# A graph network layer on one core: another order of columns for the product of W2 and x

## The chip, the cores and the metric

The kernel runs on one core of one Trainium2 chip. The metric is the device time of one execution in microseconds (us); lower is better.

## The reference, cut to what matters

```python
def _bn(h, gamma, beta):
    mu = jnp.mean(h, axis=0, keepdims=True)
    var = jnp.mean((h - mu) ** 2, axis=0, keepdims=True)
    return (h - mu) * jax.lax.rsqrt(var + EPS) * gamma + beta
row, col = (edge_index[0], edge_index[1])
h = jnp.concatenate([x[row], edge_attr], axis=1)
h = jax.nn.relu(_bn(h @ W1 + b1, g1, be1))
s = jax.ops.segment_sum(h, col, num_segments=n)
agg = jnp.where(cnt > 0, s / jnp.maximum(cnt, 1.0), 0.0)
h2 = jnp.concatenate([x, agg], axis=1)
h2 = jax.nn.relu(_bn(h2 @ W2 + b2, g2, be2))
return jax.nn.relu(h2 @ Wl + bl)          # then: layernorm(x + this)
```

x is 3125 x 128 (nodes), there are 53125 edges with 64 attributes each, sorted by destination, W1 is 192 x 128, W2 is 256 x 256 and Wl is 256 x 128, all in float32. The first 128 rows of W2 meet x, the last 128 meet the mean over edges. The part of the product with x does not depend on the edges at all, so it can be made at any time.

## The kernel before, in words

The edges are cut into 104 groups of 512 (4 tiles of 128). Four groups make a step, so there are 26 steps (i = 0 to 25). A first pass over the 26 steps makes h @ W1 for every edge and the sums for the first norm; a second pass applies the norm's shift and relu and sums into the nodes; a last part does the node layer. This change touches only the first pass.

**One step i of the first pass.** GpSimd (POOL, function `gather`, line 682) fetches rows of the table x @ W1 from DRAM, one indirect DMA for each tile of 128 edges. In group q = 2 three of the four tiles are not fetched but picked by TensorE, so a step from i = 1 on has 13 indirect DMAs and not 16. Before the gathers of group g, GpSimd waits until h of group g - 4 is made (`pool.wait_ge(h_ready, g - 3)`), so it may run at most four groups ahead of the groups that VectorE finishes. GpSimd has nothing else in this pass.

TensorE (PE, function `edge_step`) issues, in this order: the edge product of group 1 (line 766); five products of one-hot matrices with the node table (`pick`, line 784, ten matmuls each), of which the first stands ahead of the change's matmul and the second right behind it; **the x product** (`x_product`, line 847) in steps 1 to 14; the edge products of groups 2 and 3; the counts (line 839), which wait until ScalarE has copied the x product out (they use the same PSUM bank `psT[1]`); the last pick; and `rows_back` (line 793), which adds the picked rows into group 2. Before `rows_back` ScalarE must copy the picked rows out of PSUM (line 1084).

VectorE (DVE) makes h of each group from the product and the gathered rows (line 1306; lines 1303 and 1304 for group 2), adds it to a running sum (line 1327), adds its squares (line 1334), makes three of the five one-hot matrices of a step (line 1319) and the small one-hots for the counts (line 1284).

ScalarE (ACT) squares h of each group (line 1031), makes the other two one-hot matrices of a step (lines 1094, five times, and 1097; `node_hot`), copies the x product out (`x_product_out`, line 1045), starts its DMA to DRAM (line 1047), places counts (line 1059) and copies the picked rows (line 1084).

**The x product.** `xt0` holds x turned, 128 features on the partitions and 3125 columns. They lie as 25 blocks t of 125 columns p (node number = 25 p + t). The result is wanted in node order, p outer and t inner. `XSTEPS` has 14 pieces: 7 ranges of p (six of 20 and one of 5) for each of the 2 halves of W2. A piece has 20 x 25 = 500 columns (5 x 25 = 125 in the last two). A float32 matmul shows as two records in the profile. The pieces are read again from DRAM in the last part.

```python
XP = 20
XSTEPS = [(h, k, min(XP, PN - k)) for k in range(0, PN, XP) for h in range(H2)]
xtv = xt0.rearrange("f (t p) -> f t p", t=NT)      # NT = 25, PN = 125
h2x = agg[:, 3 * GF:3 * GF + XW]                   # XW = 500
```

`psT`, `psH`, `psC`, `psS` and `psX` are PSUM banks; `agg`, `res` and `work` are places in SBUF that several things share.

Of the kernel before, what the change touches and what calls it, by code (L numbers as in the profile page):

```python
# [31 lines left out]
ACT = mybir.ActivationFunctionType  # L32
AX_X = mybir.AxisListType.X

P = 128
# [21 lines left out]
def gnn_kernel(nc, E, x, xt, src, src_rows, dst, dst_rows, ea, W1, b1, g1, be1, W2, b2, g2, be2, Wl, bl, out):  # L57
# [3 lines left out]
    NT = 25  # L61
# [25 lines left out]
    with ctx:  # L87
# [3 lines left out]
        def pb(name, shape):  # L91
            return ctx.enter_context(nc.psum_tensor(name, shape, F32))

        def sem(name):
            return ctx.enter_context(nc.semaphore(name))
# [116 lines left out]
        w2x = agg[:, 0:H2 * P]  # L212
        h2x = agg[:, 3 * GF:3 * GF + XW]
# [5 lines left out]
        psT = [pb(f"psT{i}", [P, 512]) for i in range(2)]  # L219
# [73 lines left out]
        x_ps = sem("w2_x_psum")  # L293
        x_out = sem("w2_x_copied")
# [84 lines left out]
        def slot(i, par, q):  # L379

            return resg(i, q) if q < KEEP else away[par][:, (q - KEEP) * GF:(q - KEEP + 1) * GF]
# [350 lines left out]
        def _(pe):  # L732
# [7 lines left out]
            xtv = xt0.rearrange("f (t p) -> f t p", t=NT)  # L740

            LISTS = len(BATCH) - 1
            for b, (t0, n) in enumerate(BATCH):
# [7 lines left out]
                for t in range(n):  # L751
                    last = pe.matmul(psY[b % len(psY)][0:PN, t * F:(t + 1) * F], xtv[:, t0 + t, :], w1x[:, :],
                                     start=True, stop=True)
# [89 lines left out]
            def x_product(m):  # L843

                h, k, n = XSTEPS[m]
                pe.wait_ge(cnt_placed, m + 1)
                pe.matmul(psT[1][:, 0:n * NT].rearrange("o (p t) -> o p t", t=NT), w2x[:, h * P:(h + 1) * P],  # L847
                          xtv[:, :, k:k + n].rearrange("f t p -> f p t"), start=True, stop=True).then_inc(x_ps, 1)

            def edge_step(i, par, nth):  # L850
                product(i, par, nth, 1)
                if i in NODES:
                    pick(i, 0)
                if i <= len(XSTEPS):
                    x_product(i - 1)
                if i in NODES:
                    pick(i, 1)
                product(i, par, nth, 2)
                if i in NODES:
                    pick(i, 2)  # L860
                    pick(i, 3)
                product(i, par, nth, 3)
                counts(i, par)
                if i in NODES:
                    pick(i, 4)
                    rows_back(i)
                if i + 1 < NI:
                    product(i + 1, 1 - par, (i + 1) // 2 + 1, 0)
# [32 lines left out]
            for j in range(TILES):  # L901
                h = slot(NI - 1, 1, U - 1)[:, j * F:(j + 1) * F]
# [31 lines left out]
            with pe.Else():  # L934
# [3 lines left out]
                          stop=True).then_inc(g_base, 1)  # L938
                with pe.Fori(0, NG) as g:
                    with pe.Fori(0, NB) as b:  # L940
                        pe.wait_ge(g_m, g + 1)
                        pe.wait_ge(g_hot, NB * g + b + 1)
                        for j in range(TILES):
                            pe.matmul(psH[0][:, 0:WIDE], mx[:, 0, j * F:(j + 1) * F], ghot[:, j * WIDE:(j + 1) * WIDE],
                                      start=(j == 0), stop=(j == TILES - 1))
# [8 lines left out]
            for h in range(H2):  # L954
                last = pe.matmul(psX[:, 2 * F + h:2 * F + h + 1], w2[:, h * P:(h + 1) * P], c(C_U), start=True,
                                 stop=True)
            last.then_inc(s_w2s, 1)
            prods = [(n, h) for n in range(NC) for h in range(H2)]
            for k, (n, h) in enumerate(prods):
# [5 lines left out]
                if k >= len(BANK):  # L965
                    pe.wait_ge(s_h2, k - len(BANK) + 1)
                pe.matmul(BANK[k % len(BANK)][:, 0:cw], w2[:, h * P:(h + 1) * P], agg[:, c0:c0 + cw], start=True,
                          stop=True).then_inc(s_h2ps, 1)
# [12 lines left out]
            for b, (t0, n) in enumerate(BATCH):  # L981
                pe.wait_ge(s_h2r, b + 1 if b < DVE_RELU else H2 * (b + 1) - DVE_RELU)
                pe.wait_ge(s_h2rd, min(b + 1, DVE_RELU))
                for t in range(n):
                    o = BANK[b][0:PN, t * F:(t + 1) * F]
                    for h in range(H2):
                        n0 = h * N + (t0 + t) * PN
                        last = pe.matmul(o, h2r[:, n0:n0 + PN], wl[:, h * F:(h + 1) * F], start=False,
                                         stop=(t == n - 1 and h == H2 - 1))
# [4 lines left out]
        def _(act):  # L994
# [44 lines left out]
            def x_product_out(m):  # L1039

                h, k, n = XSTEPS[m]
                act.wait_ge(x_ps, m + 1)
                if m:
                    act.wait_ge(x_saved, 16 * m)
                act.activation(h2x[:, 0:n * NT], psT[1][:, 0:n * NT], ACT.Copy).then_inc(x_out, 1)
                act.wait_ge(x_out, m + 1)
                act.dma_start(h2x_dram[:, h, k * NT:(k + n) * NT], h2x[:, 0:n * NT]).then_inc(x_saved, 16)

# [50 lines left out]

            node_hot(NODE0, 0)  # L1100
            x_product_out(0)
            node_hot(NODE0, 1)
            for i in range(1, NI - 1):
                squares(i, 0)
                place_counts(i)
                if i in NODES:
                    rows_out(i)
                squares(i, 1)
                hot_out(i + 1, (i + 1) % 2)
                if i + 1 in NODES:  # L1110
                    node_hot(i + 1, 0)
                squares(i, 2)
                if i < len(XSTEPS):
                    x_product_out(i)
                squares(i, 3)
                if i + 1 in NODES:
                    node_hot(i + 1, 1)
# [503 lines left out]
```

## Time and profile before

| what | value |
|---|---|
| runs of the kernel before | 586.23, 587.31, 763.84 us (median 587.31) |
| the profiled execution's own time | 585.97 us |
| its span | 584.2 us |
| PE busy | 527.9 us (90%) |
| PE weight load busy | 464.9 us (80%) |
| DVE busy | 509.0 us (87%) |
| ACT busy | 425.3 us (73%) |
| POOL busy | 362.0 us (62%) |
| first pass | to about 443 us |

The profiled execution took 1.8 us more than its span, which is what lies around the program. Two of the three runs stand within 1.4 us of it; the third is far off and is not used. The busy shares are averages over three very different parts; the first pass must be read by its own rows. Engines are named as in the profile: PE is TensorE, PEld its weight load, DVE VectorE, ACT ScalarE, POOL GpSimd.

### The profile page before, as it was taken

The numbers are of one execution on the slowest core, as the hardware profiler recorded it, in microseconds if no ns is written. First come the engines' busy times: TensorE is split into PE (matmuls) and PEld (weight loads), VectorE is DVE, ScalarE is ACT, GpSimd is POOL, SyncE is SP. The second block draws the span as 40 slices with busy tenths as digits, with TensorE's granted clock in tenths as the row PEclk, the third lists the DMA queues.
The fourth block names the chain that finished last, engine by engine and source line by source line (L and its number), as shares of the span: only waits on it lengthen the run. The fifth ranks groups of instructions, "written<-read, shape, count | busy, mean of one in ns | idle before, by whom it ended". The sixth has DMA issues, their size and how long they took to land.

```text
span 584.2 us, 10621 instructions
## 1 busy us (share of the span) xinstructions
PE 527.9 (90%) x3099; PEld 464.9 (80%) x3099; DVE 509.0 (87%) x719; ACT 425.3 (73%) x850; POOL 362.0 (62%) x464
## 2 busy tenths in 40 slices
PE   3679999999999999999999988898997999999993
PEld 4658878877778878888888877787885999999583
DVE  5796999999999999999999989898986877777787
ACT  2458777887788777888888877678767566666476
POOL 4776777777777777777777777777770333333500
PEclk9789999999999999999999999899999999999997
DMA  7844454455444554444444444354345688775004
GB/s 197 263 142 125 158 161 143 133 162 167 155 140 146 163 166 141 140 145 139 143 145 148 145 150 148 109 148 150 95 121 164 219 252 267 251 253 169 1 1 111
DMA packets 48139, 90.21 MB, mean 154 GB/s; under 512 B 10885, under 2 KB 30260, under 8 KB 48099
## 3 DMA queue, kind: packets, MB, share of 16 engines
q1 hardware_dynamic: 30734, 59.97, 31.2%
q0 software_dynamic: 10912, 22.37, 15.0%
q10 hardware_dynamic: 6453, 7.38, 3.6%
q8 instruction: 19, 0.31, 0.2%
q14 instruction: 21, 0.17, 0.1%
HBM read 66.71 MB, written 22.97 MB: 153 GB/s over the span
## 4 chain that ended last, share of the span: by engine, by line
PE 55%; DVE 20%; issue 8%; POOL 8%; ACT 4%; DMA 3%; DVEq 0%; ACTq 0%; POOLq 0%
PE psT L784 22%; PE psH L923 8%; PE psC L923 8%; POOL res L682 6%; DVE node_hot L1319 6%; PE psH L766 5%; PE psT L847 4%; DVE psX L1334 3%; PE psC L766 2%; DVE res L1306 2%; PE psH L793 1%; DMA res<-ytab,srci 1%; DVE res L1473 1%; POOL res L666 1%; ACT node_rows_turned L1084 1%
## 5 line engine op out<-in xcount | busy, mean ns | idle before, releaser
L682 POOL DMA_INDIRECT res<-ytab,srci x265 | 250.2, 944 | 81.8 <-issue 77.1
L784 PE MATMUL psT<-node_hot,node_table 125*128 125x384 f32 x1250 | 261.9, 358 | 4.5 <-DVE node_hot L1319 3.7
L784 PEld LDWEIGHTS psT<-node_hot,node_table 125*128 125x128 f32 x1250 | 222.3, 191 | 29.5 <-issue 12.5
L1319 DVE TENSOR_TENSOR node_hot<-agg,psC 125x1920 fp32r<-125x1920 int32 x75 | 161.0, 2147 | 0.0
L1094 ACT ACTIVATE node_hot<-agg,nodeid 125x384 fp32r<-125x384 int32 x250 | 131.8, 603 | 8.8 <-PE psT L784 6.6
L1097 ACT ACTIVATE node_hot<-node_hot,ones 125x1920 fp32r<-125x1920 f32 x50 | 95.1, 1902 | 1.6
L1435 DVE TENSOR_TENSOR work<-res,psX 128x512 f32<-128x512 f32 x104 | 70.8, 687 | 20.2 <-PE psH L923 10.1
L707 POOL TENSOR_TENSOR agg<-agg,srci 128x64 f32 x104 | 32.0, 308 | 74.6 <-ACT srci L1161 55.0
L766 PE MATMUL psH<-w1e,work 128*128 128x256 f32 x268 | 70.5, 385 | 6.0 <-DVE res L1304 3.3
L682 POOL DMA_INDIRECT work<-ytab,srci x64 | 60.7, 948 | 23.7 <-issue 16.8
L1334 DVE TENSOR_TENSOR psX<-agg,psX 128x512 f32<-128x512 f32 x103 | 71.1, 690 | 4.4 <-ACT agg L1031 4.3
L766 PEld LDWEIGHTS psH<-w1e,work 128*128 128x128 f32 x268 | 47.6, 189 | 16.0 <-DVE res L1304 7.0
L1031 ACT ACTIVATE agg<-res 128x512 f32<-128x512 f32 x77 | 47.5, 618 | 15.1 <-DVE res L1306 7.7
L1327 DVE TENSOR_TENSOR psS<-res,psS 128x512 f32<-128x512 f32 x77 | 53.6, 696 | 2.7
L923 PE MATMUL psH<-work 128*128 128x128 f32 (+1 forms) x416 | 51.9, 279 | 1.0 <-DVE work L1435 1.0
L923 PE MATMUL psC<-work 128*128 128x128 f32 (+1 forms) x416 | 51.2, 277 | 0.0
L923 PEld LDWEIGHTS psH<-work 128*128 128x128 f32 x416 | 49.6, 196 | 1.2 <-DVE work L1435 1.2
L923 PEld LDWEIGHTS psC<-work 128*128 128x128 f32 x416 | 49.1, 194 | 0.0
L766 PE MATMUL psC<-w1e,work 128*128 128x256 f32 x132 | 35.0, 387 | 3.2 <-DVE res L1304 2.3
L1059 ACT ACTIVATE cnt<-psT 1x64 f32 x104 | 22.4, 215 | 20.4 <-PE psT L839 17.6
L1306 DVE TENSOR_TENSOR res<-psH,res 128x512 f32<-128x512 f32 x42 | 28.7, 683 | 2.7 <-DMA res<-ytab,srci 2.4
L766 PEld LDWEIGHTS psC<-w1e,work 128*128 128x128 f32 x132 | 23.5, 189 | 8.2 <-DVE res L1304 4.1
(222 smaller groups left out, 534.8 us busy)
## 6 DMA issues: line engine op xcount, KB each, us to landing
work<-in_edge_attr SPq DMA_DIRECT2D x26, 512.0 KB, 3.6
res<-spill SPq DMA_DIRECT2D x25, 512.0 KB, 3.6
spill<-work SPq DMA_DIRECT2D x13, 512.0 KB, 2.8
spill<-res SPq DMA_DIRECT2D x12, 512.0 KB, 2.9
agg<-in_src_rows SPq DMA_DIRECT2D x25, 192.0 KB, 3.9
res<-ytab,srci POOLq DMA_INDIRECT x265, 2.6
res<-h2x_dram SPq DMA_DIRECT2D x10, 312.5 KB
h2x_dram<-agg ACTq DMA_DIRECT2D x12, 250.0 KB
```

The costliest lines, as they stand in the source:

```text
L682: pool.indirect_dma_start(rows[:, j * F:(j + 1) * F], None, ytab, bass.IndirectOffsetOnAxis(ap=srci[:, j, g:g + 1], axis=0)).then_inc(gath ...
L766: last = pe.matmul(psP[g % len(psP)][:, b * 2 * F:(b + 1) * 2 * F], ea_cols(par, q, b), w1e[:, :, :].rearrange("p a f -> p (a f)"), start= ...
L784: last = pe.matmul(rows_at, table[0:PN, part, (t0 + t) * F:(t0 + t + 1) * F], hot_now[0:PN, t, :], start=(n == 0 and t == 0 and part == 0) ...
L923: last = pe.matmul(psA[q][:, 0:n], mx[:, q, j * F:(j + 1) * F], hotf[:, q, j * WIN:j * WIN + n], start=(j == 0), stop=(j == TILES - 1))
L1031: act.activation(sq[g % 2], slot(i, i % 2, q), ACT.Square).then_inc(sq_ready, 1)
L1094: act.activation(hots[2][0:PN, t, :], rows[i % 2][0:PN, :].bitcast(I32), ACT.Abs, bias=nodeid[0:PN, t0 + t:t0 + t + 1], scale=-1.0).then_i ...
L1097: act.activation(hots[2][0:PN, :, :], hots[2][0:PN, :, :], ACT.Relu, bias=ones[0:PN, :], scale=-1.0).then_inc(hot_by_act, 1)
L1306: dve.tensor_tensor(h, ps[:, :], h, ALU.add).then_inc(h_ready, 1)
L1319: dve.tensor_tensor(dve_hot(i, d)[0:PN, :, :], rows[i % 2][0:PN, :].bitcast(I32).unsqueeze(1).broadcast_to([PN, CUT, HOTW]), nodep[:, t0:t ...
L1327: last = dve.tensor_tensor(psS[:, :], slot(i, par, q), psS[:, :], ALU.add)
L1334: last = dve.tensor_tensor(psX[:, :], sq[g % 2], psX[:, :], ALU.add)
L1435: dve.tensor_tensor(tiles(mx[:, q, :]), tiles(hin), negu, ALU.max).then_inc(m_ready, 1)
```

## The change

TensorE now reads the columns of a piece in the order in which they lie: for each block t a run of 20 neighbouring columns (80 bytes), where before it took one column of every block (500 bytes apart) and then the next. The matmul writes PSUM without gaps as before, but in the order t outer, p inner. ScalarE's copy out of PSUM now reads every 20th column of PSUM (every 5th in the last two pieces) and writes node order without gaps to SBUF. The data that reach DRAM, all waits, all semaphores and the order of the instructions on every engine are the same.

```diff
-                pe.matmul(psT[1][:, 0:n * NT].rearrange("o (p t) -> o p t", t=NT), w2x[:, h * P:(h + 1) * P],
-                          xtv[:, :, k:k + n].rearrange("f t p -> f p t"), start=True, stop=True).then_inc(x_ps, 1)
+                pe.matmul(psT[1][:, 0:n * NT].rearrange("o (t p) -> o t p", t=NT), w2x[:, h * P:(h + 1) * P],
+                          xtv[:, :, k:k + n], start=True, stop=True).then_inc(x_ps, 1)
```

```diff
-                act.activation(h2x[:, 0:n * NT], psT[1][:, 0:n * NT], ACT.Copy).then_inc(x_out, 1)
+                act.activation(h2x[:, 0:n * NT].rearrange("o (p t) -> o p t", t=NT),
+                               psT[1][:, 0:n * NT].rearrange("o (t p) -> o p t", t=NT), ACT.Copy).then_inc(x_out, 1)
```

## Rows read from the trace of the kernel before

**Rows 1.** Chain of waits, 100 to 270 us: start us, us, what.
```profile
107.07 1.88 PE psT L847 x2
...
123.45 1.88 PE psT L847 x2
...
235.96 0.69 DVE psX L1334
...
244.61 1.13 DVE hotb L1284
...
259.69 1.12 DVE work L1284
```
**Rows 2.** L847 against L888 by source line: ns min/median/max, first and last start us.
```profile
L847 PE MATMUL psT<-res,agg x28: 397/1102/1122, 41.3 to 253.4; 128*128 128x500 f32 x24, 128*128 128x125 f32 x4
...
L888 PE MATMUL psT<-cnt,work x10: 379/592/595, 436.8 to 442.2; 128*128 128x512 f32 x8, 128*128 128x256 f32 x2
```
**Rows 3.** Chain of waits, 395 to 470 us.
```profile
399.40 3.53 DMA res<-ytab,srci
...
422.98 1.13 PE psC L766 x4
...
436.96 0.86 PE psT L888 x2
```
**Rows 4.** Timeline of POOL: start us, us, instruction, [idle before <-releaser].
```profile
55.17 0.94 POOL L682 DMA_INDIRECT work<-ytab,srci  x1 [0.89 <-DVE res L1304]
59.16 0.94 POOL L682 DMA_INDIRECT work<-ytab,srci  x1 [3.05 <-DVE res L1306]
...
75.57 0.94 POOL L682 DMA_INDIRECT res<-ytab,srci  x1 [0.48 <-DVE work L1306]
...
254.55 0.94 POOL L682 DMA_INDIRECT work<-ytab,srci  x1 [0.30 <-DVE res L1306]
...
438.12 0.94 POOL L682 DMA_INDIRECT res<-ytab,srci  x1 [0.30 <-issue]
```
**Rows 5.** L682 alone in two stretches: us, then POOL busy (instructions).
```profile
59.00:254.50 195.50, 146.31 (x155) 1.00 0.49 152
254.50:438.20 183.70, 138.84 (x148) 0.99 0.45 138
```
**Rows 6.** Chain of waits, 270 to 440 us.
```profile
325.75 0.94 POOL res L682
```
**Rows 7.** Timeline of ACT in steps 1 and 5, and PE's last pick of step 5.
```profile
40.59 1.90 ACT L1097 ACTIVATE node_hot<-node_hot,ones 125x1920 fp32r<-125x1920 f32 x1
...
108.99 0.59 ACT L1045 ACTIVATE agg<-psT 128x500 f32<-128x500 f32 x1 [1.25 <-PE psT L847]
...
109.98 0.63 ACT L1031 ACTIVATE agg<-work 128x512 f32<-128x512 f32 x1 [0.40 <-ACT agg L1045]
...
110.75 2.65 ACT L1094 ACTIVATE node_hot<-agg,nodeid 125x384 fp32r<-125x384 int32 x5
...
113.43 1.90 ACT L1097 ACTIVATE node_hot<-node_hot,ones 125x1920 fp32r<-125x1920 f32 x1
...
116.11 2.01 PE L784 MATMUL psT<-node_hot,node_table 125*128 125x384 f32 x10
```
**Rows 8.** Two reads of a full PSUM bank by DVE, strided and not (L1340, L1327).
```profile
L1340 DVE TENSOR_REDUCE work<-psS x1: 684/684/684, 439.6 to 439.6; 128x128 f32<-128x512 f32 x1
...
L1327 DVE TENSOR_TENSOR psS<-res,psS 128x512 f32<-128x512 f32 x77 | 53.6, 696 | 2.7
```
**Rows 9.** Timeline of PE in two late steps.
```profile
358.03 1.13 PE L766 MATMUL psH<-w1e,work 128*128 128x256 f32 x4 [1.34 <-DVE work L1304]
358.81 3.86 PE L784 MATMUL psT<-node_hot,node_table 125*128 125x384 f32 x20
...
374.96 1.37 PE L766 MATMUL psC<-w1e,work 128*128 128x256 f32 x4 [2.08 <-DVE res L1304]
375.76 5.40 PE L784 MATMUL psT<-node_hot,node_table 125*128 125x384 f32 x20
```
**Rows 10.** Windows: us, PE, PEld, DVE, ACT, POOL busy (x), then PEclk.
```profile
376.00:380.00 4.00, 4.00 (x16) 3.91 (x16) 3.96 (x5) 1.14 (x2) 3.09 (x4) 0.61 0.25 61
```

## The prediction

> **What bounds the kernel now.** I read the chain of waits first, since it tells which engine sets the pace where, and not over all. From 38 to about 235 us it is PE from end to end, and in each step it holds 1.88 us of the x product; one x product starts 16.38 us after the other [rows 1]. From 236 us on, where the x products have shrunk to 125 columns and then stop, the chain changes to DVE, and a step takes 259.69 - 244.61 = 15.08 us [rows 1]. From 325.75 us it goes through POOL's indirect DMAs [rows 6], and it leaves them only with the gather of 399.40 us, whose data arrive 3.53 us later [rows 3]. So there are three paces, and the third decides the end of the pass.
>
> Next I read POOL's timeline, because an engine that feeds a pass of 26 equal steps can be its pacer even where the chain does not show it. From 254.55 us to the last gather at 438.12 us [rows 4] there are 148 gathers [rows 5], so 147 intervals in 183.57 us: 1.249 us each, with no stall. 13 gathers make a step: 16.23 us. That is almost the 16.40 us of the PE steps, and more than the 15.08 us of the DVE steps. What POOL has done ahead is used up between 236 and 326 us: 6 steps x (16.23 - 15.08) = 6.9 us of lead. After that POOL paces the pass.
>
> How long does POOL stand still before? From the gather at 59.16 us to the last there are 155 + 148 = 303 gathers [rows 5], 302 intervals, 302 x 1.249 = 377.1 us unhindered. It took 438.12 - 59.16 = 378.96 us. So POOL stalls by only 1.8 us in all, in about eleven waits for h of four groups earlier; one is [rows 4] at 75.57 us, 0.48 us in place of the usual 0.30. Ahead of that are two start-up stalls, at 55.17 us (0.89 - 0.30 = 0.6 us) and at 59.16 us (3.05 - 0.30 = 2.7 us) [rows 4].
>
> **The change part by part.** *The matmul.* The two records of a 500-column product take 1102 ns each; the nearest contiguous float32 row is 128x512 at 592 ns [rows 2]. In the chain, where overlap is taken off, that is 1.88 us for 500 columns [rows 1] against 0.86 us for 512 [rows 3], or 0.84 us for 500. The new product lies between 0.84 us (as good as contiguous) and 1.88 us (no gain). I take 0.90 us, near the contiguous row, since runs of 20 columns have only 25 jumps in 500. Saved on PE: 0.98 us in each of 12 pieces, 11.8 us in sum; the last two pieces have 125 columns and lie where DVE sets the pace, so they count nothing.
>
> The Trainium skill (SBUF — State Buffer, section "Door 1: The DMA port swizzle") says that SBUF is read in lines of 16 bytes and that each element on a new line costs extra; the 500-byte steps of before would pay it each time, and runs of 80 bytes once in four or so. That agrees in direction with the two durations of rows 2, and a line or two more per run would put the product nearer 1.0 than 0.84 us, which changes nothing in the sum below.
>
> *ScalarE's copy.* Before it takes 0.59 us [rows 7]. The trace has no strided read of PSUM by ACT. The nearest is DVE's: a sum that reads a bank with jumps of 128 columns takes 684 ns, the plain one 696 ns [rows 8]; by this the copy stays at 0.59 us. The other bound is the matmul's own factor, 1.88/0.84 = 2.2, so 1.32 us. I take 0.6 us. What is behind it on ACT: the DMA start, the square of group 3, then the second one-hot matrix (110.75 and 113.43 us), which PE's last pick needs at 116.11 us. The square ends at 110.61 us, 0.14 us before the one-hot work starts, which waits for PE's pick; the one-hot ends at 115.33 us, 0.8 us before the pick [rows 7]. So 0.9 us more on the copy is hidden while PE's step is the bound, and more once it isn't. DVE needs the square only two microseconds after its end. If the cover goes, the price must first exceed the 0.98 us that the matmul gives back: 0.9 + 0.98 = 1.9 us more than now before a step is longer than today's.
>
> The same page and section says that PSUM's lines are 8 bytes and that a non-contiguous access slows matmuls much. That speaks for the upper bound, if it holds for a reader that is not TensorE; no row here shows it for ACT, and by the cover just worked out a copy of 1.32 us gives the same sum.
>
> *What of the 11.8 us reaches the end.* PE's step falls to 16.38 - 0.98 = 15.4 us, still above DVE's 15.08 us but now below POOL's 16.23 us. So POOL's waits vanish (1.8 us), its lead of about 6.9 us shrinks by 0.83 us in each step, and after some 8 steps, near 190 us, PE and DVE wait for gathered rows. From there the pass runs at POOL's pace to the end. The only other gain is at the start: the gather of 59.16 us waits for h of group 3 of step 1, which stands behind the first x product. That product ends at 41.3 + 2.04 = 43.3 us; the pick behind it needs ACT's one-hot, which ends at 40.59 + 1.90 = 42.49 us [rows 2, 7]. So the first piece brings only 0.7 us and not 0.98. Sum: 0.7 + 1.8 = **2.5 us** earlier last gather (435.6 us), and the rest of the pass and the program with it. The other 9.3 us turn into waits of PE and DVE.
>
> Against the profiled execution: 585.97 - 2.5 = 583.5 us. The two close runs are 586.23 and 587.31 us, so the same sum gives 583.7 and 584.8. I say 584.0 us. The change moves it by 0.4%, and a change within 2% (about what a measurement of this kernel can tell from no change) is what I expect to be seen.
>
> **The rivals.** *PE's whole saving arrives* (the pass follows PE, POOL could go faster if asked). For it: the chain names PE in most of the pass. Against: 147 gathers without a stall at 1.249 us. It would give 585.97 - 11.8 = 574.2 us.
>
> *The product gets no faster*: its 1102 ns come from something other than the jumps in its reads. Against it: same type, nearly same columns, half the time in [rows 2]. Time 586 to 587 us.
>
> *The clock (the slower side).* Once PE waits for gathers, its gaps grow. After a gap of 1.34 us, 20 picks took 3.86 us; after one of 2.08 us they took 5.40 us [rows 9] at a granted clock of 0.61 [rows 10], so part of them at the lower of the two levels, 1.2 GHz. Price: about 1.55 us per event, and some 17 steps will now be paced by POOL and not 5. Mostly it is hidden, since a PE step without x product has 1 to 2 us to spare against 16.23; it counts if a drop comes in the last two steps (1.5 us), or if it comes in every second step and the cheap steps between (15.08 us) do not make it up: (16.23 + 0.3 + 1.55 + 15.08)/2 = 16.6 us, 0.35 x 15 = 5 us lost, less the 2.5 gained: 588.5 us. It decides from one drop in every two steps on.
>
> *ACT's copy is far dearer*, above 2.5 us. At 4 us each: (3.4 - 1.9) x 12 = 18 us longer, 604 us. No row is near it.
>
> **How the numbers follow.** Forecast 0.72, whole saving 0.05, no faster product 0.08, clock 0.12, dear copy 0.03. The forecast's own spread is that of the runs and of a drop near the end, 582 to 586; no faster product and most of the clock case reach to 587.5. I give 581.5 to 587.5, leaving out the whole saving, the dear copy and the worst of the clock. Faster by over 2% (below some 575): 0.03, most of the whole-saving case, whose forecast lies just on that line. Slower by over 2%: 0.02. Within: 0.95.
>
> **What would show it.** Right: records of the x product near 600 ns; PE steps of 15.4 us between 60 and 190 us; POOL without a DVE wait over 0.30 us after the gather of 58.4 us, and its last gather at 435.6 us; from about 190 us on DVE's and PE's waits for gathered rows in every step. Wrong: POOL gathers closer than 1.249 us; a last gather that moves with PE's 11.8 us; a copy above 1.5 us with ACT in the chain; a granted clock that falls every other step with the end of the pass behind 441 us.

## The result and the profile after

The changed kernel takes 582.74 us (median of nine runs), the kernel before 585.9 us in the same comparison. The ratio is 0.9944, with a 95% interval of 0.993 to 0.9957: 3.3 us less, between 2.5 and 4.1. The forecast of 584.0 us was 1.3 us too high, and its gain of 2.5 us stands at the small end of the interval; 0.6 us of the 1.3 lie in the time of the kernel before, which the forecast took from higher runs (585.9 - 2.5 = 583.4 us). Medians count every run, also the few that lie far off (763.84 us among these nine of the kernel before, 660.76 us for one kernel below), so where median and ratio disagree, the ratio counts. The profiled execution took 583.22 us with a span of 581.5, 2.75 us less than the one before.

The product itself, by source line (ns min/median/max, first and last start in us), against [rows 2]:

```profile
L847 PE MATMUL psT<-res,agg x28: 276/596/1040, 40.5 to 245.5; 128*128 128x500 f32 x24, 128*128 128x125 f32 x4
```

The median record fell from 1102 to 596 ns; a contiguous product of 512 columns took 592. Only the longest is nearly as long as before (1040 ns), and it belongs to the first piece. The copy by source line:

```profile
L1045 ACT ACTIVATE agg<-psT x14: 277/588/590, 42.4 to 245.8; 128x500 f32<-128x500 f32 x12, 128x125 f32<-128x125 f32 x2
```

588 ns as before: reading every 20th column of PSUM costs ScalarE nothing for a piece of 500. (For the two pieces of 125, whose copy reads every fifth column, the minimum went from 252 to 277 ns, and nobody waits for that.) The rule of the Trainium skill on short PSUM lines (SBUF — State Buffer, section "Door 1: The DMA port swizzle") is written for matmuls; no cost of that kind is in the 500-column copy.

Where the time went is in the chain of waits of the changed kernel, 30 to 300 us (start us, us, what), against [rows 1]:

```profile
40.71 1.67 PE psT L847 x2
...
57.12 0.87 PE psT L847 x2
...
72.52 0.87 PE psT L847 x2
...
87.86 0.87 PE psT L847 x2
...
165.83 0.94 POOL res L682
...
185.80 2.48 DMA res<-ytab,srci
```

The x product holds 0.87 us of a step where it held 1.88, and a step of PE takes 87.86 - 72.52 = 15.34 us and not 16.38. But from about 166 us on the chain runs through POOL's gathers and their landing, where before it got there at 326 us [rows 6]. The timeline of POOL, against [rows 4]:

```profile
58.45 0.95 POOL L682 DMA_INDIRECT work<-ytab,srci  x1 [2.56 <-DVE res L1307]
...
435.50 0.94 POOL L682 DMA_INDIRECT res<-ytab,srci  x1 [0.30 <-issue]
```

and the gathers alone in that stretch (us, then POOL busy and instructions), against [rows 5]:

```profile
58.40:435.60 377.20, 285.13 (x303) 1.00 0.47 146
```

303 gathers start in 435.50 - 58.45 = 377.05 us, so 1.249 us apart without a stall. Before, the same 303 took 378.96 us. The last gather is 2.6 us earlier (435.50 against 438.12), and behind it the program is as long as before: 581.5 - 435.5 = 146.0 us against 584.2 - 438.1 = 146.1. So in these two executions the end of the program moved with the last gather. (Over the profiled executions below that have all these gathers, the stretch behind the last one varies from 144.9 to 147.3 us.) The other part of what TensorE saved is now waiting, as a late step shows (timeline of PE):

```profile
355.54 1.13 PE L766 MATMUL psH<-w1e,work 128*128 128x256 f32 x4 [1.47 <-DVE work L1305]
...
372.17 1.13 PE L766 MATMUL psC<-w1e,work 128*128 128x256 f32 x4 [1.78 <-DVE res L1305]
```

### The profile page after: what moved, and what is told of

Its sections match the earlier page's. It is cut to its first block, busy times and chain, and to the rows that moved or that the text cites. A ratio compares the mean times of both kernels' runs of the same rounds, so it can differ in the third digit from the quotient of the medians.

```text
span 581.5 us, 10621 instructions
## 1 busy us (share of the span) xinstructions
PE 514.3 (88%) x3099; PEld 461.6 (79%) x3099; DVE 509.3 (88%) x719; ACT 425.7 (73%) x850; POOL 362.0 (62%) x464
## 4 chain that ended last, share of the span: by engine, by line
PE 41%; POOL 20%; DVE 15%; issue 12%; DMA 8%; ACT 3%; DVEq 0%; ACTq 0%; POOLq 0%
POOL res L682 17%; PE psT L784 14%; PE psC L923 8%; PE psH L923 8%; DMA res<-ytab,srci 6%; DVE node_hot L1320 4%; PE psH L766 3%; DVE psX L1335 2%; DVE res L1307 2%; POOL work L682 1%; PE psT L847 1%; DVE res L1474 1%; POOL res L666 1%; PE psH L793 1%; PE psC L766 1%
## 5 line engine op out<-in xcount | busy, mean ns | idle before, releaser
L682 POOL DMA_INDIRECT res<-ytab,srci x265 | 250.4, 945 | 80.8 <-issue 76.2
L784 PE MATMUL psT<-node_hot,node_table 125*128 125x384 f32 x1250 | 254.8, 352 | 5.5 <-DVE node_hot L1320 4.7
L682 POOL DMA_INDIRECT work<-ytab,srci x64 | 60.4, 943 | 22.1 <-issue 18.6
```

Source lines behind the costliest of these rows:

```text
L682: pool.indirect_dma_start(rows[:, j * F:(j + 1) * F], None, ytab, bass.IndirectOffsetOnAxis(ap=srci[:, j, g:g + 1], axis=0)).then_inc(gath ...
L784: last = pe.matmul(rows_at, table[0:PN, part, (t0 + t) * F:(t0 + t + 1) * F], hot_now[0:PN, t, :], start=(n == 0 and t == 0 and part == 0) ...
```

## The experiments

**A wider lead for the gathers.** If the change gained by taking POOL's stalls away, then letting POOL run one group further ahead must gain the same without the change, and with it the change must be worth nothing.

```diff
-                    pool.wait_ge(h_ready, g - 3)
+                    pool.wait_ge(h_ready, g - 3 if g < 8 else g - 4)
```

Expected of the kernel before with this:

> The kernel before, but GpSimd may gather five groups ahead of the groups that VectorE has finished and not four (from group 8 on). Theory (GpSimd's gathers pace the pass, and the change gained by taking their stalls away): the stalls of 0.6, 2.7 and 1.8 us go without the faster product, the last gather starts near 433.5 us and not 438.1, and the time falls by about 4.6 us to 581.3. Rival (the gain comes from TensorE's shorter product as such): nothing changes, 585.9 us.

And of the changed kernel:

> The same wider lead in the changed kernel. Theory: the last gather starts near 433.5 us as in the kernel before with the wider lead, the time is 580.6 to 581.3 us, and the faster product is worth nothing on top of the wider lead (under 0.7 us). Rival: it keeps its 3 us, so about 3 us less than the kernel before with the wider lead.

Measured: 582.28 us (ratio 0.9931, 0.9919 to 0.9944) and 581.85 us (0.9923, 0.9906 to 0.994), the kernel before at 586.11. The last gathers by source line, first without and then with the change:

```profile
L682 POOL DMA_INDIRECT res<-ytab,srci x265: 940/944/1018, 29.1 to 434.0; - x133
```

```profile
L682 POOL DMA_INDIRECT res<-ytab,srci x265: 940/944/1913, 28.4 to 433.8; - x133
```

They start at 434.0 and 433.8 us, 0.5 and 0.3 us later than worked out. The faster product is worth 0.4 us on top of the wider lead, inside the intervals; the rival's 3 us are excluded. The time of the first came out 1.0 us above the figure given. Part of it is in its profile: GpSimd still waits for VectorE three times, between 201 and 236 us, 0.4 us in all, where the figure had nothing. The rest has no shown place. One changed number in a wait brings as much as the change does, and both together give the lowest time of a kernel that computes everything, though its interval overlaps that of the change alone.

**One gather less in a step.** Now the other way round: take POOL off the bound and see whether the rest of TensorE's saving comes out. Group 1 of steps 2 to 25 is gathered without tile 0, and VectorE fills that tile from the product alone.

```diff
+def fewer(i, q):
+
+    return 1 if i >= 2 and q == 1 else 0
...
-                for j in range(node_tiles(i) if q == NODEQ else 0, TILES):
+                for j in range(node_tiles(i) if q == NODEQ else fewer(i, q), TILES):
...
+                if fewer(i, q):
+                    dve.tensor_tensor(h[:, F:GF], ps[:, F:GF], h[:, F:GF], ALU.add)
+                    dve.tensor_copy(h[:, 0:F], ps[:, 0:F]).then_inc(h_ready, 1)
+                    return
```

> The kernel before without the gather of tile 0 of group 1 in steps 2 to 25, whose h is then the edge product alone (that part of x @ W1 is left out): 12 gathers a step, 15.0 us of GpSimd. VectorE gets one short instruction more, about 0.1 us a step. Theory: without GpSimd as the pacer of the late steps the pass follows TensorE (16.4 us a step) and then VectorE (15.2 us): about 6 us less than before, 580 us. Rival (GpSimd is not what paces the late steps): 585 to 587 us.

> The same left out of the changed kernel. Theory: TensorE's steps of 15.4 us now reach the end, so the faster product is worth 10 to 12 us here, about 569 us, against 3 us with all gathers. Rival (the other 9 us are lost in TensorE itself, its clock or ScalarE's copy): the difference to the kernel before with 12 gathers stays near 3 us.

Measured: 580.85 us without the change (ratio to the kernel before 0.9904, 0.9884 to 0.9924) and 569.01 us with it (0.9713, 0.9697 to 0.9728). With 12 gathers a step the same two edits are worth 11.8 us (each of the two times is known to about 1 us), with 13 gathers 3.3 us. The chain without the change (60 to 450 us):

```profile
205.31 1.88 PE psT L852 x2
...
221.69 1.88 PE psT L852 x2
...
395.78 1.12 DVE hotb L1289
...
410.92 1.12 DVE work L1289
```

and with it:

```profile
195.64 0.87 PE psT L852 x2
...
211.04 0.87 PE psT L852 x2
...
384.12 1.12 DVE hotb L1290
...
399.25 1.13 DVE work L1290
```

Steps of 16.38 us become 15.40 us, both kernels then go over to VectorE's steps of 15.14 us, and neither chain goes through a gather in the late steps. This is the run that settles the cause: nothing in TensorE, in its clock or in the copy holds the bulk of the saving back.

**Only the first piece, and all but the first.** In both, `if m == 0` or `if m > 0` chooses between the new and the old form of product and copy.

> Only the first of the 14 pieces in the new way (product and copy), the others as before. Theory: GpSimd's eleven small stalls stay (1.8 us), only the start-up stall can shrink, by at most 0.7 us: 585.2 to 586.1 us, the last gather at 437.4 us or later. Rival (each shorter product brings its 0.98 us): 585.1 us, which this run cannot tell from the theory; the next one can.

> All pieces but the first in the new way. Theory: the small stalls of 1.8 us go, the start-up stall stays: 1.8 to 2.5 us less than before, 583.6 to 584.3 us, and 0 to 0.7 us more than the changed kernel. Rival (a gain in proportion to the pieces, 1/12 of it for each): 583.0 us.

Measured: 585.77 us (0.999, 0.9978 to 1.0002) and 583.01 us (0.9948, 0.9928 to 0.9967), the kernel before at 586.22. The first piece alone gains between -0.1 and 1.3 us, which can be told neither from nothing nor from the forecast's 0.7 us; all but the first bring the whole gain within the intervals. The stretch of 303 gathers fits too: 437.88 - 59.03 = 378.85 us with the first piece alone, 435.01 - 57.99 = 377.02 us with all others. The second median is 0.6 us below its range.

The first piece brought little for a reason that the forecast had not seen. In step 1 TensorE comes out of a wait for its first one-hot (3.66 us in the kernel before, 3.92 us in the changed one), and in the profiled execution of the changed kernel the first product runs at a low clock (windows; us, PE busy, PEclk):

```profile
36.00:40.00 4.00, 2.83 (x9) 0.50 0.46 126
40.00:44.00 4.00, 4.00 (x14) 0.65 0.22 61
44.00:48.00 4.00, 4.00 (x24) 1.00 0.39 114
```

A granted clock of 0.50 is the lower level, 1.2 GHz. There the new product takes 1.67 us, hardly less than the old one's 1.88. Not every execution is like that, as the new product with the old copy shows further down.

**Nearly no product.** In every piece the matmul has 25 columns, which ScalarE's copy spreads over 500; most of W2's product with x is left out.

```diff
-                pe.matmul(psT[1][:, 0:n * NT].rearrange("o (t p) -> o t p", t=NT), w2x[:, h * P:(h + 1) * P],
-                          xtv[:, :, k:k + n], start=True, stop=True).then_inc(x_ps, 1)
+                pe.matmul(psT[1][:, 0:25], w2x[:, h * P:(h + 1) * P],
+                          xtv[:, 0, 0:25], start=True, stop=True).then_inc(x_ps, 1)
```

> The changed kernel with an x product of 25 columns in every piece, spread over the 500 by ScalarE's copy (it leaves out nearly all of W2's product with x), so TensorE's step falls to about 14.6 us. Theory: the pass stays at GpSimd's pace and nothing is gained beyond the changed kernel but up to 0.7 us at the start: 582.0 to 582.7 us. Rival (the pass follows TensorE or VectorE where the trace names them): 8 us less, since 12 steps could fall from 15.4 to VectorE's 15.1 us and POOL's pace did not bind.

Measured: 585.58 us (0.9975, 0.9958 to 0.9992). Neither was right: by the ratios it is 1.8 us slower than the changed kernel, with less work. The profiled execution's span is 2.8 us longer, 584.3 against 581.5 us. Its timeline of PE in step 1:

```profile
41.09 0.46 PE L847 MATMUL psT<-res,agg 128*128 128x25 f32 x2
42.17 3.57 PE L784 MATMUL psT<-node_hot,node_table 125*128 125x384 f32 x10 [0.62 <-ACT node_hot L1098]
45.54 1.68 PE L766 MATMUL psH<-w1e,work 128*128 128x256 f32 x4
```

and the windows of the same stretch:

```profile
40.00:44.00 4.00, 3.38 (x13) 0.50 0.27 82
44.00:48.00 4.00, 4.00 (x16) 0.64 0.29 80
```

The small product leaves a hole of 0.62 us, the granted clock stays at 0.50 through 44 us, and ten picks take 3.57 us where they took 2.70 in the changed kernel. The gather behind the start-up stall starts at 60.45 us and not at 58.45, and the last at 437.54 us: 377.09 us between them, as in the changed kernel. So nothing was lost between them. But the 2.0 us at the start are not all the hole's: the first pick of step 1 started 0.59 us later in this execution (37.76 against 37.17 us), and from it to the gather are 22.69 us against 21.28, so step 1 itself lost 1.4 us. The last 0.8 us of the longer span lie behind the last gather. To test whether the start is the cause, the first piece was given back:

> As the run with a tiny product in every piece, but the first piece is the changed kernel's own. In that run step 1 held a hole on TensorE behind the tiny product, the granted clock stayed low to about 46 us, and the gather after the start-up stall came at 60.45 us in place of 58.45. Theory (that start is all that cost it 2.8 us, and from there GpSimd's 377 us follow): with a full first product the start is the changed kernel's, the gather after the stall comes near 58.5 us, the last one near 435.6 us, the time is 582.2 to 583.3 us. Rival (tiny products in the steps behind cost time by the clock or by waits): 585 us again.

Measured: 584.27 us (0.9968, 0.9955 to 0.9982), the kernel before at 586.79 in that comparison. The absolute figure is above the range, and the ratio does not differ clearly from that of the run before. But the new product with all its columns and the plain copy, timed beside it, has 584.40 us. So near each other, they say what the first question asked: beside a whole product of the new kind, a tiny one in 13 pieces is worth nothing. The profile has the start where the theory put it or better, with step 1's windows at 0.50, 0.81 and 1.00. (Its first pick also started early, at 36.27 us; from there to the gather are 21.07 us.)

```profile
57.34 0.95 POOL L682 DMA_INDIRECT work<-ytab,srci  x1 [1.05 <-DVE res L1315]
...
435.09 0.95 POOL L682 DMA_INDIRECT res<-ytab,srci  x1 [0.30 <-issue]
```

Here the 303 gathers took 377.75 us, without a stall, 1.251 us apart and not 1.249. That 0.2% of GpSimd's own pace shows at the end as 0.7 us. So the profiled executions show that a full first product gives step 1 that time back. That this is why the times of the kernel with only tiny products are higher is not shown: with the first piece given back the ratio hardly moved.

**The two halves of the change.**

> The new product with the old plain copy (the order of part of the output is changed). Theory: the copy costs nothing, so 582.7 us as with both, and ScalarE's copy takes 588 ns as it does with both. Rival (the strided copy costs and is paid from the gain): less than 582 us.

> The old product with the new strided copy (the order of part of the output is changed). Theory: 585.9 us as before, the product's records stay at 1102 ns (it is the read from SBUF and not the place or order in PSUM), the copy takes 588 ns. Rival: above 586.5 us, or a copy longer than 0.6 us.

Measured: 584.40 us (0.9963, 0.9948 to 0.9978) and 586.13 us (0.9998, 0.9984 to 1.0012), the kernel before at 586.79. The copy alone changes nothing, and the product alone gives the gain but for an amount inside the intervals (the 582.7 us expected of it is 1.7 us too low, of which 0.9 are in the kernel before of that comparison). The new product with the old copy also shows what the first piece can bring. In its profiled execution the low level ended before most of the first product (windows of 0.76 and 0.82, like the 0.72 and 0.85 of the kernel before):

```profile
40.97 1.27 PE L847 MATMUL psT<-res,agg 128*128 128x500 f32 x2
42.24 2.03 PE L784 MATMUL psT<-node_hot,node_table 125*128 125x384 f32 x10
...
58.34 0.94 POOL L682 DMA_INDIRECT work<-ytab,srci  x1 [2.15 <-DVE res L1306]
```

ScalarE's one-hot ends at 42.20 us there and the pick behind the product starts at 42.24, so the one-hot is what limits the gain, as the forecast had it. From the first pick (37.82 us) to the gather are 20.52 us, 0.64 us less than before.

The product by source line with the new copy alone:

```profile
L847 PE MATMUL psT<-res,agg x28: 397/1102/1122, 40.1 to 252.3; 128*128 128x500 f32 x24, 128*128 128x125 f32 x4
```

and the copy of that kernel:

```profile
L1045 ACT ACTIVATE agg<-psT x14: 277/588/591, 42.3 to 245.8; 128x500 f32<-128x500 f32 x12, 128x125 f32<-128x125 f32 x2
```

**How long must a run be?**

```diff
+        RUNS = [20, 20, 1, 1, 2, 2, 4, 4, 5, 5, 10, 10]
...
+                pe.matmul(psT[1][:, 0:n * NT].rearrange("o (a t b) -> o a t b", t=NT, b=run), w2x[:, h * P:(h + 1) * P],
+                          xtv[:, :, k:k + n].rearrange("f t (a b) -> f a t b", b=run), start=True, stop=True
```

> The kernel before with x read in runs of 20 columns (pieces 0 and 1), 1 (2, 3), 2 (4, 5), 4 (6, 7), 5 (8, 9) and 10 (10, 11); the copy is the plain one, so part of the order of the output is changed. If a read costs by jumps to another line of memory, a record takes about 600 ns for runs of 20 and 10, 1100 ns for 1 and something between for 2; if it is enough that two neighbouring columns are read together, runs of 2 already take 600 ns. If the jumps were not the cause, all stay at 1100 ns or all at 600 ns.

Timeline of PE, one of each pair (the two records together): runs of 20, 1, 2, 4, 5 and 10 columns.

```profile
57.62 1.03 PE L849 MATMUL psT<-res,agg 128*128 128x500 f32 x2
...
73.00 2.04 PE L849 MATMUL psT<-res,agg 128*128 128x500 f32 x2
...
105.82 1.31 PE L849 MATMUL psT<-res,agg 128*128 128x500 f32 x2
...
137.14 1.13 PE L849 MATMUL psT<-res,agg 128*128 128x500 f32 x2
...
168.06 1.07 PE L849 MATMUL psT<-res,agg 128*128 128x500 f32 x2
...
198.93 1.01 PE L849 MATMUL psT<-res,agg 128*128 128x500 f32 x2
```

Twenties and tens as fast as contiguous, single columns slow and pairs between: that is the first of the three forms, by jumps to another line. But the price is not in proportion to the number of jumps. Most of it goes with the first neighbour: from 2.04 us with single columns to 1.31 us with pairs (8 bytes); fours take 1.13 us, tens 1.01 us, and twenties no less. All pieces share one output form, so the reads alone make the difference. The one execution of this kernel took 582.71 us, near the changed kernel's 582.74, with six of its pieces slower than the change's, and its 303 gathers took 377.06 us, without a stall: the waits leave room for slower products. One execution cannot say more about the time.

## Why the prediction was right

**What paces the pass: right.** The three paces (TensorE 16.4 us a step, VectorE 15.1, GpSimd 16.23) were read before the change, and the run with 12 gathers shows what happens when the third is taken away: 11.8 us out of the same edits, against the 11.8 us that the forecast gave as the sum over 12 pieces of 0.98 us. That the two agree to the tenth is luck, with times known to 1 us. One reading was loose: the chain before is not PE from end to end. In each step about 1.3 us of it are ScalarE's copy of the picked rows (0.50 us) and VectorE's h of group 2 (lines 1303 and 1304, 0.77 us). The step of 16.38 us holds them, so the sum does not change.

**The matmul and the copy: right.** 0.87 us against the 0.90 taken; 588 ns against 0.6 us. PE's steps are 15.34 us where 15.4 was forecast.

**The stalls: right.** The forecast took 1.8 us for the eleven small ones. Measured are 378.96 - 377.05 = 1.9 us, and all variants with the new product in the later pieces have 377.0 to 377.1, but for the one execution with GpSimd's slower pace (377.75).

**Where the lead is used up: near.** Forecast near 190 us, seen in the chain from 166 us on, with a first wait for a landing at 188 us.

**The first piece: right at one clock, nothing at the other.** "So the first piece brings only 0.7 us and not 0.98" took for granted that the first product runs at the higher clock. In the one profiled execution where the new product mostly did, the one with the old copy, it brought 0.64 us, by the way that the forecast gave. In the other six with a new first piece the low clock reached over the product, which took 1.67 us in each. Leaving out the wider lead, where GpSimd has no such wait, from the first pick to the gather are 21.1 to 21.5 us in these, against 21.1 to 21.3 us with an old first piece: no gain. The profile of after does show its start-up gather 0.71 us earlier, just as worked out, but for another reason: its first pick started at 37.17 us in place of 38.00. From that pick to the gather are 21.28 us, and 21.16 before. In the other profiled executions that first pick starts anywhere from 36.27 to 37.89 us, old and new first pieces mixed. So the last gather's 435.5 us against the forecast's 435.6 is in part luck. A number that fits is not yet a cause.

**What stays open.** Stalls of 1.9 us and little for the first piece make about 2 us, and the interval begins at 2.5. The rest, half a microsecond or more, has no shown place; the start of the pass varies by more than that from one execution to the next, and so does the stretch behind the last gather.

**The rivals.** The whole saving did not arrive (574.2 us) while POOL has 13 gathers. The clock did not fall in the changed kernel's late steps, though PE waited up to 1.78 us there, and over 1.3 us in about half of the steps (all windows from 180 us on have 1.00); a gap of 1.99 us in the kernel with tiny products was followed by 20 picks in 4.83 us, like the one of 2.08 us in [rows 9]. From the end of that gap to the last of the 20 picks are 6.25 us, against 4.61 us behind the gap of 1.47 us in the changed kernel: 1.6 us, and the forecast's price was 1.55. The changed kernel's gaps stayed shorter than the two that were followed by a drop.

## What to carry to other kernels

Before pricing a saving on the engine that the chain names, count what every other engine issues in one step of the loop and multiply by its spacing when nothing stops it: here 13 x 1.249 us left 0.15 us of the 1.04 us by which a step became shorter. The gain that reaches the end is then the stalls of the second pacer, and a wait that limits how far it may run ahead may give the same for one number in the code. Change the bound by itself (one gather less) to see whether the rest of the saving is there.

## What the runs showed of the hardware

A float32 product read at 500-byte steps costs 1.88 us for 500 columns, and the cost is in the read: pairs of neighbours take away most of it, runs of ten all. At half the granted clock the old read takes no longer, while a record of the new one goes from 596 to 1040 ns: the single-column read is not limited by TensorE's clock. The kernel before with the wider lead shows it, first the product in its timeline of PE, in step 1:

```profile
40.97 2.06 PE L847 MATMUL psT<-res,agg 128*128 128x500 f32 x2
```

and the window of the same two microseconds:

```profile
41.00:43.00 2.00, 2.00 (x4) 0.50 0.12 35
```

2.06 us at a clock of 0.50, and 2.04 us at full clock in the timeline of runs above (73.00 us). ScalarE reads PSUM at 80-byte steps as fast as without gaps, 588 ns for 128x500. And less work on TensorE can make a step longer: in the profiled execution with a first product cut to 0.46 us the clock stayed at its lower level for some 4 us more (to about 46.9 us where it was 42.8, by the shares of the windows above, and 41.0 to 43.9 in the other eleven executions), and from the first pick to the steady gathers it took 1.4 us more. That is one execution.
